# Graph layer with relation weights: three of every 66 gather tiles fetched row by row instead of two, with byte offsets and 32 registers per load

## The chip, the cores and the metric

The kernel runs on one core of a Trainium2 chip. Its time is the device time of one launch, in microseconds: the median of three runs of the kernel before is 10409.57 us (10406.67 to 10411.6). The profiled execution of the same kernel took 10414.85 us.

## The reference

A graph has 12,500 nodes of 64 features and 412,500 edges, sorted by destination; every edge has one of 65 types. A first layer sums normalised source rows per destination. Then the relational part runs twice:

```python
seg = dst * r + edge_type
msg = x[src]
agg = segment_sum(msg, seg).reshape(n, r, d)
mean = agg / maximum(cnt, 1.0)
out = einsum('nrd,rdk->nk', mean, W_r) + x @ W_root + b
h = relu(out) + relu(h @ res_W + res_b)
```

The kernel multiplies first and gathers afterwards: for every node it writes the rows of x W_r for all 65 types (and the root and residual products) into a table in HBM, `y_table`. An edge then needs one row of 64 floats (256 bytes) of this table, at row `src * 67 + type`. A one-hot matrix weighted by 1/count adds the rows of a tile of 128 edges into their destinations on TensorE.

## The kernel before, in words

There are three passes: `l = 0` is the first graph layer, `l = 1` and `l = 2` are the gather passes of the two relational layers. The change concerns `l = 2`, which here is called layer 2 (`ROW_LAYER = 2`). In it nothing is multiplied by relation weights any more; it only gathers and sums.

The edges are cut into 98 steps (`S = 98`) of 33 tiles (`T = 33`), a tile being 128 edges. A step has three groups (`J = 3`, index `j`) of 11 tiles (`K = 11`, index `k`). Two steps make a pair, `i` is the pair, `u = 0` or `1` the step within it, and all engines loop over pairs. The buffers of `u = 0` are called `rows` in the trace, those of `u = 1` lie in a weight buffer and are called `w_parts`. So there are six groups of buffers, and each group is refilled once in a pair.

- GpSimd (POOL) fetches tiles: one `indirect_dma_start` (line 878) takes 128 rows by the indices in `idx_st`. It may fill a group's buffers when TensorE is through with them (`agg_done`) and the indices lie ready (`idx_staged`).
- One tile in each step, the last one of the first group (`j = 0`, `k = ROW_K = 10`), is not fetched by GpSimd (`pool_tiles`). Its 128 indices are loaded into one partition (`load_row_idx`, line 299). Then SyncE (SP) or ScalarE (ACT) reads 16 of them into registers (line 305, a TENSOR_LOAD) and issues 16 transfers of one row each (line 309), and so on (`load_rows`). SP does this for the tile of `u = 0`, half of it in either step of the pair; ACT does it for the tile of `u = 1`, in the same way.
- ACT also copies the sums of the step before out of PSUM (line 987), and stages the indices for GpSimd two steps ahead (line 982, `stage_ahead`), each group when TensorE has used the group's buffers.
- TensorE (PE, line 1436) waits for a group's gathers and, at the row-by-row tile, for `rows_landed`; then it does 11 matmuls, which the trace counts as 22 since they are of f32. After a step's first group it turns the sums of the step before (line 1270), and VectorE (DVE) finishes that block (lines 1675 to 1684).
- SP also loads the root and residual product of each block (`load_rr`, line 563).

SP's queue for one pair (`sp_step`) is: load the row indices of the next pair; load `rr`; wait for the first group of this step and for the indices; 64 rows; `rr`; 64 rows. ACT's (`act_step`) is, in each step: copy the sums, then stage and issue rows in turn, 64 rows a step.

Of the kernel before, what the change touches and what calls it, by code (L numbers as in the profile page):

```python
# [5 lines left out]
P = 128  # L6
# [39 lines left out]
def gnn_kernel(nc, N, E, R, D, x, src, dst, etype, rel_W, root, bias, res_W, res_b,  # L46
# [4 lines left out]
    f32, bf16, i32 = mybir.dt.float32, mybir.dt.bfloat16, mybir.dt.int32  # L51
# [10 lines left out]
    J = 3  # L62
# [22 lines left out]
    ROW_BATCH = 16  # L85
    ROW_HALF = P // 2

# [31 lines left out]
    with ctx:  # L119
# [172 lines left out]
        row_idx = [extra[0:1, u * P:(u + 1) * P] for u in range(2)]  # L292

        def pool_tiles(l, j, tiles):
            return [k for k in range(tiles) if not (l == ROW_LAYER and j == 0 and k == ROW_K)]

        def load_row_idx(eng, pair, u):
            at = (pair * 2 + u) * T + ROW_K
            eng.dma_start(row_idx[u].rearrange("p (e a) -> p e a", a=1),
                          col_table[1:2, :, bass.ds(at, 1)], allow_slow_non_contiguous=True)\  # L300
               .then_inc(row_idx_loaded[u], 16)

        def load_rows(eng, which, l, u, r0, n):
            for c0 in range(r0, r0 + n, ROW_BATCH):
# [107 lines left out]
        rows_landed = [sem(f"rows_landed{u}") for u in range(2)]  # L412
        row_idx_loaded = [sem(f"row_idx_loaded{u}") for u in range(2)]
# [65 lines left out]
        def _(sp):  # L479
# [101 lines left out]
            with sp.If(in_windows == 1):  # L581
# [53 lines left out]
                for l in (1, 2):  # L635
# [11 lines left out]
                    if l == ROW_LAYER:  # L647
                        wait_alone(sp, agg_done[l], 1)
                        load_row_idx(sp, 0, 0)
                        wait_alone(sp, row_idx_loaded[0], 16)  # L650
                        load_rows(sp, mybir.EngineType.SP, l, 0, 0, P)

                    def sp_step(i, u, more):
# [6 lines left out]
                        def next_rows(n):  # L660
                            if more:
                                load_rows(sp, mybir.EngineType.SP, l, 0, u * ROW_HALF + n * ROW_BATCH, ROW_BATCH)

                        if more and u == 0:
                            load_row_idx(sp, i + 1, 0)
# [5 lines left out]
                        if more and u == 0:  # L671
                            wait_alone(sp, agg_done[l], s * J + 2 * J + 1)
# [1321 lines left out]
```

## Time and profile before

| | |
|---|---|
| median of three runs | 10409.57 us |
| the profiled execution | 10414.85 us, of which the span of the program is 10412.8 us |
| POOL busy | 7664.3 us, 74% |
| DVE, PE, ACT busy | 52%, 44%, 22% |
| DMA in layer 2 | 16% of the 16 engines' time, 30 GB/s |
| layer 2 | from 6497 us to the end |

A POOL row of the profile is 0.94 us long and another follows 0.30 us later, without pause; this gap is shown as "issue", time in which the engine waits for nothing that the trace records. Instructions that set registers, branch, wait on a semaphore or issue a transfer are not counted as busy, so an engine can have its queue full and look idle. They do have records, under SPq and ACTq (the queues of SyncE and ScalarE); FUSED_REGOPS is register arithmetic, MOVE sets one register, DMA_DIRECT2D issues one transfer and TENSOR_LOAD reads memory into registers.

### The profile page before, as it was taken

The numbers are of one execution on the slowest core, as the hardware profiler recorded it, in microseconds if no ns is written. First come the engines' busy times: TensorE is split into PE (matmuls) and PEld (weight loads), VectorE is DVE, ScalarE is ACT, GpSimd is POOL, SyncE is SP. The second block draws the span as 40 slices with busy tenths as digits, with TensorE's granted clock in tenths as the row PEclk, the third lists the DMA queues.
The fourth block names the chain that finished last, engine by engine and source line by source line (L and its number), as shares of the span: only waits on it lengthen the run. The fifth ranks groups of instructions, "written<-read, shape, count | busy, mean of one in ns | idle before, by whom it ended". The sixth has DMA issues, their size and how long they took to land.

```text
span 10412.8 us, 180513 instructions
## 1 busy us (share of the span) xinstructions
PE 4552.2 (44%) x39273; PEld 3351.5 (32%) x39273; DVE 5439.9 (52%) x20234; ACT 2260.0 (22%) x5671; POOL 7664.3 (74%) x8196
## 2 busy tenths in 40 slices
PE   4489898885444444444444444222222222222222
PEld 3366666663222222222222222122222222222222
DVE  9877676766766766766776776222222222222222
ACT  7756565652111111111111111000000000000000
POOL 6577777775777777777777776777777777777777
PEclk8889999996666666666666666555555555555555
DMA  3234444445444444444444444111111111111112
GB/s 88 60 129 147 139 147 140 146 138 166 147 146 138 146 142 142 146 141 144 142 143 145 140 144 146 30 30 30 30 30 30 30 30 30 30 30 30 30 30 41
DMA packets 517848, 1018.14 MB, mean 98 GB/s; under 512 B 224773, under 2 KB 270869, under 8 KB 516309
## 3 DMA queue, kind: packets, MB, share of 16 engines
q1 hardware_dynamic: 242628, 745.04, 19.6%
q0 software_dynamic: 254784, 263.18, 13.0%
q14 instruction: 662, 5.42, 0.2%
q10 hardware_dynamic: 19600, 1.66, 0.1%
q8 instruction: 174, 2.85, 0.1%
HBM read 559.40 MB, written 454.23 MB: 97 GB/s over the span
## 4 chain that ended last, share of the span: by engine, by line
POOL 60%; issue 23%; PE 8%; DVE 4%; SPq 2%; ACT 1%; DMA 1%; POOLq 0%; ACTq 0%; DVEq 0%
POOL rows L878 33%; POOL w_parts L878 27%; PE y_ps L1241 3%; PE block_ps L1328 2%; DVE ystage L1569 2%; SPq L309 1%; PE sums_ps L1293 1%; PE y_ps L1320 1%; ACT scr L1016 1%; SPq L305 0%; PE signs_ps L1320 0%; DMA y_table<-ystage 0%; ACTq L309 0%; DVE onehot L1604 0%; DMA rows<-h_table,idx_st 0%
## 5 line engine op out<-in xcount | busy, mean ns | idle before, releaser
L878 POOL DMA_INDIRECT rows<-y_table,idx_st x3185 | 3009.1, 945 | 1052.4 <-issue 1051.8
L878 POOL DMA_INDIRECT w_parts<-y_table,idx_st x3163 | 2986.9, 944 | 964.5 <-issue 964.5
L1675 DVE TENSOR_SCALAR rr<-rr 128x64 f32<-128x64 f32 x198 | 43.4, 219 | 4125.0 <-PE block_ps L1270 4125.0
L1436 PE MATMUL sums_ps<-onehot,rows 128*64 128x64 f32 x6468 | 762.2, 315 | 2669.9 <-DMA rows<-y_table,idx_st 2537.8
L1436 PE MATMUL sums_ps<-w_parts 128*64 128x64 f32 x6424 | 754.6, 315 | 2583.7 <-DMA w_parts<-y_table,idx_st 2505.4
L878 POOL DMA_INDIRECT rows<-h_table,idx_st x1452 | 1399.0, 964 | 552.6 <-issue 453.5
L1436 PEld LDWEIGHTS sums_ps<-onehot,rows 128*64 128x64 f32 x6468 | 710.7, 225 | 2748.8 <-issue 1320.4
L1436 PEld LDWEIGHTS sums_ps<-w_parts 128*64 128x64 f32 x6424 | 707.4, 225 | 2658.0 <-issue 2169.1
L982 ACT ACTIVATE idx_st<-edges 128x11 int32 (+1 forms) x720 | 141.3, 210 | 5850.9 <-PE sums_ps L1436 3218.2
L1006 ACT ACTIVATE ystage<-y_ps 128x512 f32<-128x512 f32 (+1 forms) x1782 | 1010.7, 568 | 977.5 <-PE y_ps L1241 819.6
L1614 DVE TENSOR_SCALAR_CACHE_REDUCE w_raw<-edges,step_key 128x384 bf16<-128x384 f32 x1568 | 850.8, 606 | 15.6 <-DVE step_key L1594 15.6
L1241 PE MATMUL y_ps<-scr,hT 128*128 128x512 bf16 (+1 forms) x2673 | 741.0, 421 | 64.8 <-ACT hT L992 54.4
L1606 DVE TENSOR_SCALAR onehot<-iota,step_rel,step_val 128x64 f32<-128x64 bf16 x3234 | 755.4, 335 | 21.9 <-PE sums_ps L1260 5.0
L1606 DVE TENSOR_SCALAR w_parts<-iota,step_rel,step_val 128x64 f32<-128x64 bf16 x3234 | 755.8, 339 | 12.3
L1241 PE MATMUL y_ps<-w_parts,hT 128*128 128x512 bf16 (+1 forms) x2673 | 705.8, 375 | 36.2 <-ACT ystage L1006 18.6
L1328 PE MATMUL block_ps<-edges,scr 128*128 128x192 bf16 x5346 | 602.2, 251 | 0.0
L1328 PEld LDWEIGHTS block_ps<-edges,scr 128*128 128x128 bf16 x5346 | 540.9, 139 | 174.9 <-issue 16.4
L1614 DVE TENSOR_SCALAR_CACHE_REDUCE w_raw<-w_raw,step_key 128x384 bf16<-128x384 f32 x784 | 425.2, 607 | 0.0
L1241 PEld LDWEIGHTS y_ps<-scr,hT 128*128 128x128 bf16 x2673 | 253.2, 111 | 528.0 <-issue 224.9
L1016 ACT ACTIVATE scr<-y_ps 128x396 bf16<-128x396 f32 x864 | 385.5, 498 | 129.2 <-PE y_ps L1320 115.4
L970 ACT ACTIVATE ystage<-iota,w_parts 128x128 bf16<-128x128 bf16 x1176 | 343.7, 385 | 3.0 <-PE signs_ps L1213 2.8
L1569 DVE TENSOR_TENSOR ystage<-t_ps,edges 128x896 bf16<-128x896 bf16 x588 | 343.9, 665 | 0.7 <-DVE win_cnt L1559 0.4
(230 smaller groups left out, 6414.8 us busy)
## 6 DMA issues: line engine op xcount, KB each, us to landing
y_table<-ystage SPq DMA_DIRECT2D x396, 768.0 KB, 3.7
edges<-key_row SPq DMA_DIRECT2D x198, 832.0 KB, 6.3
y_table<-ystage SPq DMA_DIRECT2D x198, 608.0 KB, 3.3
w_parts<-y_table ACTq DMA_DIRECT2D x6272, 0.2 KB
rows<-y_table SPq DMA_DIRECT2D x6272, 0.2 KB
w_raw<-key_row SPq DMA_DIRECT2D x99, 832.0 KB, 7.1
rows<-y_table,idx_st POOLq DMA_INDIRECT x3185
w_parts<-y_table,idx_st POOLq DMA_INDIRECT x3163, 2.5
```

The costliest lines, as they stand in the source:

```text
L309: eng.dma_start(rows_of(l, u)[r:r + 1, 0, ROW_K, 0:D], y_table[l - 1][bass.ds(value, 1), :])\
L878: pool.indirect_dma_start(out=rows_of(l, u)[:, j, k, 0:D], out_offset=None, in_=table, in_offset=bass.IndirectOffsetOnAxis(ap=idx_of(l, u, ...
L970: ins = nc.scalar.activation(hist_oh[:, v, K - SIGNS + a, 0:P], iota[:, 0:P], ACT.Sign, bias=lo_half[:, bass.ds(q * SIGNS + a, 1)], scale= ...
L982: nc.scalar.activation(idx_of(l, u, j), of, ACT.Copy).then_inc(idx_staged[l], 1)
L1006: nc.scalar.activation(ystage[:, n % 2, o:o + y_cols(c)], y_ps[c % 2][:, 0:y_cols(c)], ACT.Copy).then_inc(y_read[l], 1)
L1016: nc.scalar.activation(counts_at(half, f), hist_ps[f % 2][half][:, 0:FC * NBK], ACT.Copy)\
L1241: ins = nc.tensor.matmul(y_ps[c % 2][:, 0:n], hT[:, v, a // 2, :], parts_of[l][:, a, c * BANK:c * BANK + n], start=a == 0, stop=a == 2 and ...
L1328: ins = nc.tensor.matmul(block_ps[:, 0:3 * D], counts.rearrange("p (n h) -> p h n", h=NBK)[:, b, :], h_cols[:, b, :], start=b == 0, stop=b ...
L1436: ins = nc.tensor.matmul(sums_ps[u][0:width, c:c + W], rows_of(l, u)[:, j, k, 0:width], onehot_of(l, u)[:, j, k, :], start=False, stop=False)
L1569: ins = V.tensor_tensor(hist_oh[:, v, 0:k, c0:c1].rearrange("p k (n b) -> p k n b", b=2), iota_ps[:, 0:2 * n].rearrange("p (n b) -> p n b" ...
L1606: ins = V.tensor_scalar(to, iota[:, 0:W], step_rel[:, s_par[0], at], step_val[:, s_par[0], at], ALU.is_equal, ALU.mult)
L1614: ins = V.tensor_scalar(at, key_b[j][:, k * P:(k + 3) * P], step_key[:, s_par[0], j * K + k:j * K + k + 1], None, ALU.is_equal, ALU.add, a ...
```

## The change

Three tiles per pair come row by row in layer 2: one for `u = 0` as before and two for `u = 1`, the last and the last but one of the first group (`ROW_KS`). They are numbered `n`: 0 and 1 as before, 2 is the new one. In each step SP and ACT issue 96 rows each. SP has all of `n = 0` and the first half of `n = 2`, ACT all of `n = 1` and the second half of `n = 2`.

The indices are multiplied by 256 on ScalarE beforehand (`place_rows`), and the transfers are addressed in a view of bytes, so the register that was loaded is the offset. One load fills 32 registers. SP now waits for ACT's `row_placed` where it waited for the index load, and in the pair's second step it waits for `agg_done` too. GpSimd takes the last tile of each group first, and in the very last tile only the 89 rows that are needed; both of these hold in all layers.

```diff
     ROW_K = K - 1
-    ROW_BATCH = 16
+    ROW_BYTES = 4 * D
+    ROW_BATCH = 32
     ROW_HALF = P // 2
+    ROW_STEP = 3 * ROW_BATCH
+    ROW_KS = (K - 1, K - 2)
...
+        def pool_tiles(l, u, j, tiles):
+            by_rows = ROW_KS[:1 + u] if l == ROW_LAYER and j == 0 else ()
+            return [k for k in range(tiles) if k not in by_rows]
...
+        def place_rows(n, loaded):
+            wait_alone(nc.scalar, row_idx_loaded[n], loaded * 16)
+            nc.scalar.activation(row_at[n], row_idx[n], ACT.Copy, scale=float(ROW_BYTES))\
+              .then_inc(row_placed[n], 1)
+
+        def load_rows(eng, which, l, n, r0, rows, k=ROW_K):
+            u = min(n, 1)
+            for c0 in range(r0, r0 + rows, ROW_BATCH):
                 _, values = nc.values_load_multi_w_load_instructions(
-                    row_idx[u][:, c0:c0 + ROW_BATCH], engines=[which], min_val=0, max_val=NBK * P * RX - 1,
+                    row_at[n][:, c0:c0 + ROW_BATCH], engines=[which], min_val=0,
+                    max_val=(NBK * P * RX - 1) * ROW_BYTES,
                     skip_runtime_bounds_check_because="sources are clamped to the table, types lie below R")
                 for r, value in enumerate(values, c0):
-                    eng.dma_start(rows_of(l, u)[r:r + 1, 0, ROW_K, 0:D], y_table[l - 1][bass.ds(value, 1), :])\
-                       .then_inc(rows_landed[u], 16)
+                    eng.dma_start(rows_of(l, u)[r:r + 1, 0, k, 0:D].bitcast(u8),
+                                  y_bytes[l - 1][:, bass.ds(value, ROW_BYTES)]).then_inc(rows_landed[n], 16)
...
                     def sp_step(i, u, more):
...
                         if more and u == 0:
-                            load_row_idx(sp, i + 1, 0)
+                            for n in (0, 2):
+                                load_row_idx(sp, n, i + 1, min(n, 1), ROW_KS[n // 2])
...
                         load_rr(l, s + 1, 1 - u)
-                        if more and u == 0:
-                            wait_alone(sp, agg_done[l], s * J + 2 * J + 1)
-                            wait_alone(sp, row_idx_loaded[0], i * 16 + 32)
-                        next_rows(0)
...
+                        if more:
+                            wait_alone(sp, agg_done[l], s * J + 2 * J + 1)
+                            wait_alone(sp, row_placed[2 * u], i + 2)
+                            if u == 0:
+                                load_rows(sp, mybir.EngineType.SP, l, 0, 0, ROW_STEP)
+                            else:
+                                load_rows(sp, mybir.EngineType.SP, l, 0, ROW_STEP, P - ROW_STEP)
+                                load_rows(sp, mybir.EngineType.SP, l, 2, 0, ROW_HALF, ROW_KS[1])
...
                         read_sums(l, s, 1 - u)
+                        if l == ROW_LAYER and u == 0 and more:
+                            place_rows(0, i + 2)
+                            load_row_idx(act, 1, i + 1, 1)
                         stage_ahead(0)
                         next_rows(0)
...
                         if l == ROW_LAYER and u == 0 and more:
-                            load_row_idx(act, i + 1, 1)
+                            for n in (1, 2):
+                                place_rows(n, i + 2)
+                            for n in (1, 2):
+                                wait_alone(act, row_placed[n], i + 2)
```

The start of SP's loop over pairs in layer 2, before. `edges` holds the row indices in one partition; ISA is register arithmetic or a wait's set-up:

```order
L687 ISA
L299 DMA edges<-col_table 1x128x1
L669 ISA
L563 ISA
L563 DMA rr<-y_table 128x128
L475 ISA x2
L305 TENSOR_LOAD edges
L309 ISA
L309 DMA rows<-y_table 1x64
```

The last two rows come 16 times behind each TENSOR_LOAD, which comes 8 times in the loop. The same place now, down to the second load:

```order
L701 ISA
L306 DMA edges<-col_table 1x128x1
L306 ISA
L306 DMA edges<-col_table 1x128x1
L684 ISA
L578 ISA
L578 DMA rr<-y_table 128x128
L490 ISA
L490 REGISTER_ALU
L318 TENSOR_LOAD edges
L323 DMA rows<-y_table 1x256 x32
L318 TENSOR_LOAD edges
```

The register arithmetic ahead of each row's transfer is gone, there is a second load of indices, and 32 transfers stand behind each of now 6 TENSOR_LOADs in the loop. The start of ACT's loop over pairs, now (`agg_t` takes the sums, L312 is `place_rows`, L998 stages the indices for GpSimd):

```order
L1003 ACTIVATE agg_t<-sums_ps 65x256
L490 ISA
L312 ACTIVATE edges<-edges 1x128
L306 ISA
L306 DMA edges<-col_table 1x128x1
L1140 REGISTER_ALU
L998 ISA
L998 ACTIVATE idx_st<-edges 128x11
L318 TENSOR_LOAD edges
L323 DMA w_parts<-y_table 1x256 x32
```

Before, the L987 copy was followed at once by the staging; the wait for SP's indices (L490), the multiplication and ACT's own index load now stand between them. GpSimd's loop in layer 2, where the first groups of `u = 0` and `u = 1` are the rows with 10 and 9, before them 10 and 10:

```order
L894 DMA rows<-y_table,idx_st 128x64 x10
L490 REGISTER_ALU
L894 DMA rows<-y_table,idx_st 128x64 x11
L490 REGISTER_ALU
L894 DMA rows<-y_table,idx_st 128x64 x11
L490 ISA
L894 DMA w_parts<-y_table,idx_st 128x64 x9
```

One gather in 64 has left the loop.

## Rows read from the trace of the kernel before

**Rows 1.** The page's part 4: shares of the chain of waits, by engine.
```profile
POOL 60%; issue 23%; PE 8%; DVE 4%; SPq 2%; ACT 1%; DMA 1%; POOLq 0%; ACTq 0%; DVEq 0%
```

**Rows 2.** Line 878 in layer 2: duration ns min/median/max, first and last start us.
```profile
L878 POOL DMA_INDIRECT rows<-y_table,idx_st x1568: 940/944/1028, 6498.2 to 10375.8; - x196
L878 POOL DMA_INDIRECT w_parts<-y_table,idx_st x1557: 940/944/1015, 6538.2 to 10402.1; - x195
  issue: 979.6, 3123
```

**Rows 3.** Timeline of SP's queue over a pair: start us, us, what, count.
```profile
8035.71 30.83 SPq L309 DMA_DIRECT2D rows<-y_table  x64
8066.82 0.36 SPq L563 DMA_DIRECT2D rr<-y_table  x1
8068.64 30.92 SPq L309 DMA_DIRECT2D rows<-y_table  x64
8102.57 0.61 SPq L299 DMA_DIRECT2D edges<-col_table  x1
8103.49 0.37 SPq L563 DMA_DIRECT2D rr<-y_table  x1
8115.73 4.42 SPq L309 DMA_DIRECT2D rows<-y_table  x10
```

**Rows 4.** Timeline of ACT and its queue in the same stretch.
```profile
8034.15 0.38 ACT L987 ACTIVATE agg_t<-sums_ps 65x256 f32<-65x256 f32 x1 [10.56 <-PE sums_ps L1436]
...
8035.73 6.00 ACTq L309 DMA_DIRECT2D w_parts<-y_table  x16
8048.16 0.21 ACT L982 ACTIVATE idx_st<-edges 128x11 int32 x1 [13.53 <-PE sums_ps L1436]
```

**Rows 5.** Line 309 by operation; below, who waited for its rows.
```profile
L309 ACTq FUSED_REGOPS  x6272: 37/37/37, 6500.7 to 10388.6; - x196
L309 ACTq DMA_DIRECT2D w_parts<-y_table x6272: 213/213/929, 6500.8 to 10388.8; - x196
L309 SPq FUSED_REGOPS  x6272: 37/37/47, 6501.1 to 10338.4; - x196
L309 SPq MOVE rows<-y_table x6272: 29/29/38, 6501.2 to 10338.4; - x196
L309 SPq DMA_DIRECT2D rows<-y_table x6272: 224/225/374, 6501.2 to 10338.5; - x196
...
  PE sums_ps L1436: 203.1, 10
```

**Rows 6.** Line 299, the index load: issues and the MOVEs ahead of them.
```profile
L299 SPq DMA_DIRECT2D edges<-col_table x49: 572/599/628, 6497.6 to 10261.5; - x49
L299 SPq MOVE edges<-col_table x48: 29/29/30, 6564.0 to 10261.4; - x48
```

**Rows 7.** Line 305, loads of 16 registers.
```profile
L305 ACTq TENSOR_LOAD <-edges x392: 1047/1202/4130, 6499.6 to 10381.5; - x196
L305 SPq TENSOR_LOAD <-edges x392: 1139/1230/1388, 6499.9 to 10330.5; - x196
```

**Rows 8.** Line 580, SP's load of one register.
```profile
L580 SPq TENSOR_LOAD <-flag x1: 922/922/922, 451.2 to 451.2; - x1
```

**Rows 9.** Line 1010, ACT's load of one register.
```profile
L1010 ACTq TENSOR_LOAD <-flag x1: 1127/1127/1127, 445.6 to 445.6; - x1
```

**Rows 10.** Timeline of SP's queue at the start of layer 2.
```profile
6497.62 0.60 SPq L299 DMA_DIRECT2D edges<-col_table  x1
6501.21 62.61 SPq L309 DMA_DIRECT2D rows<-y_table  x128
6564.10 0.63 SPq L299 DMA_DIRECT2D edges<-col_table  x1
```

**Rows 11.** Timeline at the end: TensorE's last group, and the last store.
```profile
10404.79 2.58 PE L1436 MATMUL sums_ps<-w_parts 128*64 128x64 f32 x22 [10.32 <-DMA w_parts<-y_table,idx_st]
...
10410.31 0.48 SPq L766 DMA_DIRECT2D out<-x_sb  x1
```

More of the change, by code:

```diff
@@ L290, in idx_of @@
             return idx_st[:, u * J + j, :]
[L292 to L299, printed above, removed]
-                          col_table[1:2, :, bass.ds(at, 1)], allow_slow_non_contiguous=True)\
-               .then_inc(row_idx_loaded[u], 16)
@@ L303, in load_rows @@
-        def load_rows(eng, which, l, u, r0, n):
-            for c0 in range(r0, r0 + n, ROW_BATCH):
+        row_idx = [extra[0:1, n * P:(n + 1) * P] for n in range(3)]
+        row_at = [extra[0:1, (3 + n) * P:(4 + n) * P] for n in range(3)]
+        y_bytes = [t.rearrange("(o n) d -> o (n d)", o=1).bitcast(u8) for t in y_table]
+        def pool_tiles(l, u, j, tiles):
+            by_rows = ROW_KS[:1 + u] if l == ROW_LAYER and j == 0 else ()
+            return [k for k in range(tiles) if k not in by_rows]
@@ L411, in gnn_kernel @@
         gathered = [[[sem(f"gathered{l}{u}{j}") for j in range(J)] for u in range(2)] for l in range(3)]
-        rows_landed = [sem(f"rows_landed{u}") for u in range(2)]
-        row_idx_loaded = [sem(f"row_idx_loaded{u}") for u in range(2)]
+        rows_landed = [sem(f"rows_landed{n}") for n in range(3)]
+        row_idx_loaded = [sem(f"row_idx_loaded{n}") for n in range(3)]
+        row_placed = [sem(f"row_placed{n}") for n in range(3)]
         idx_staged = [sem(f"idx_staged{l}") for l in range(3)]
@@ L658, in next_keys @@
                             load_keys(s * J + J + j, j)
-                        def next_rows(n):
-                            if more:
-                                load_rows(sp, mybir.EngineType.SP, l, 0, u * ROW_HALF + n * ROW_BATCH, ROW_BATCH)
                         if more and u == 0:
-                            load_row_idx(sp, i + 1, 0)
+                            for n in (0, 2):
+                                load_row_idx(sp, n, i + 1, min(n, 1), ROW_KS[n // 2])
                         if l == 1:
@@ L670, in sp_step @@
                         load_rr(l, s + 1, 1 - u)
[L671 to L674 removed]
                         if l < 2:
[L676 to L680 removed]
+                            save_y(l, s, u, range(YG - 1))
                         if l == 1:
@@ L876, in gather_group @@
                         wait_alone(pool, agg_done[l], q + 1)
-                        for k in pool_tiles(l, j, tiles):
+                        ks = pool_tiles(l, u, j, tiles)
+                        for k in ks[-1:] + ks[:-1]:
+                            n = END_ROWS if isinstance(s, int) and (s * J + j) * K + k == (E - 1) // P else P
                             pool.indirect_dma_start(
-                                out=rows_of(l, u)[:, j, k, 0:D], out_offset=None, in_=table,
-                                in_offset=bass.IndirectOffsetOnAxis(ap=idx_of(l, u, j)[:, k:k + 1], axis=0))\
+                                out=rows_of(l, u)[0:n, j, k, 0:D], out_offset=None, in_=table,
+                                in_offset=bass.IndirectOffsetOnAxis(ap=idx_of(l, u, j)[0:n, k:k + 1], axis=0))\
                                 .then_inc(gathered[l][u][j], 16)
@@ L1098, in _ @@
                     if l == ROW_LAYER:
+                        for n in (0, 2):
+                            place_rows(n, 1)
                         for slot in range(2):
@@ L1108, in act_step, with next_rows @@
                         more = not isinstance(s, int) or s + ahead < S
-                        ready = [False]
-                        def next_rows(n):
+                        def next_rows(b):
                             if l == ROW_LAYER and (more or u == 0):
-                                if u and not ready[0]:
-                                    ready[0] = True
-                                    wait_alone(act, row_idx_loaded[1], i * 16 + 32)
-                                load_rows(act, mybir.EngineType.Activation, l, 1,
-                                          (1 - u) * ROW_HALF + n * ROW_BATCH, ROW_BATCH)
+                                if u:
+                                    n, r0 = 1, b * ROW_BATCH
+                                else:
+                                    n, r0 = ((1, ROW_STEP), (2, ROW_HALF), (2, ROW_HALF + ROW_BATCH))[b]
+                                load_rows(act, mybir.EngineType.Activation, l, n, r0, ROW_BATCH, ROW_KS[n // 2])
                         def stage_ahead(j):
```

41 lines of the change are left out of this document (22 added, 19 removed).

## The prediction

> **What bounds the kernel now.** I read the page first, its shares of the chain of waits. POOL carries 60% of the span, and the 23% of "issue" are its 0.30 us pauses: nothing else matters much over the whole kernel [rows 1]. Then the one line of POOL in layer 2: 1568 + 1557 = 3125 gathers, the first starting at 6498.2 and the last ending at 10402.1 + 0.94 = 10403.0. That is 1.2495 us per gather, 64 gathers and 80.0 us per pair of steps, and of all idle time ahead of them practically everything is "issue" [rows 2]. So layer 2 is GpSimd's gather rate from end to end. Every gather less in a pair is worth 1.25 us x 49 pairs = 61.2 us, if POOL stays what comes last.
>
> Whether it stays is told by the queue that will now do more. SP's queue in one pair: 64 rows in 30.83 us, `rr`, 64 rows in 30.92, 3.0 us for the loop's return (8099.56 to 8102.57), index load, `rr`, and then nothing from 8103.86 until shortly before 8115.73 [rows 3]. The last load of registers ahead of 8115.73 took 1.2 us, so SP waited about 10.6 of 80.0 us and worked 69.4. This is the figure that the change must fit under 78.7 us (63 gathers). ACT's queue is lighter: it does the same 128 rows at 0.37 to 0.39 us each and sits waiting for TensorE before it stages indices [rows 4]. TensorE waited for rows that came one by one only 10 times, 203 us, all at the start of the layer [rows 5].
>
> **The cost of one row on SP.** From the first row at 8035.71 to the `rr` behind it at 8066.82 there are 31.11 us, with 64 rows, 3 more register loads of 1.23 us [rows 7] with a gap of 0.035, and about 0.24 for `rr`'s own registers. That leaves 27.07 us, 0.423 per row. Its parts: FUSED_REGOPS 0.037, MOVE 0.029, DMA_DIRECT2D 0.225 [rows 5], and 0.132 in three gaps of 0.044. The byte offsets take away the FUSED_REGOPS and one gap: 0.423 - 0.081 = **0.342 us**. The MOVE stays. It isn't the arithmetic: index loads have it for 48 of 49 issues, all but the first, whose address is fixed [rows 6], so it belongs to a transfer with an offset in a register, and these still have one. Bounds of the row: 0.335 from the medians alone, 0.350 if the gap that goes is a short one.
>
> **The cost of one load of 32 registers.** No row shows it. 16 registers take 1.230 us on SP and 1.202 on ACT [rows 7], one takes 0.922 on SP [rows 8] and 1.127 on ACT [rows 9]. The steeper line, SP's, adds 16 x 0.0205 = 0.33 and gives 1.56; a flat cost gives 1.23, and less than that no row gives a reason for. I take the middle, **1.39**. From the other side, if all of it were per register, it would be 2 x 1.23 = 2.46.
>
> **SP's turn over one pair, after.** In each step 96 rows: 96 x 0.342 + 3 x (1.39 + 0.035) = 37.1 us. The turn is then
> - return of the loop 3.0;
> - from the issue of the index load to the first row load 2.8: 2.3 until the indices have landed (issue at 6497.62, first register load at 6499.9 [rows 10, 7]), then ACT's new multiplication, a small activation like the 0.21 of line 982 [rows 4], with some 0.25 for two hand-overs. The second index load (0.9) and `rr` (0.65) lie inside these 2.8. Before, the landing lay under the 10.6 us of waiting; that cover is gone now;
> - 37.1, `rr` 0.7, two waits 0.2, and 37.1 again.
>
> The sum is **80.9 us**. The same sum with the old figures (3.0 + 1.3 + 0.1 + 32.1 + 0.7 + 32.1 = 69.3) gives the 69.4 measured above. So SP needs 80.9 us for what POOL now does in 63 x 1.2495 = 78.7, and 80.0 before. The likeliest outcome is that the bound moves from POOL to SP's queue and the pair gets 0.9 us longer instead of 1.25 shorter.
>
> Does anything else hold it up? ACT issues rows at (6.00 - 0.213) / 15 = 0.386 [rows 4, 5], less 0.037 and a gap of 0.036 = 0.313; three times 32 rows and a load are 34.3 us a step. In the first step of a pair ACT starts 2.8 us behind SP's index load (it must multiply it first), so its last rows of the second tile of `u = 1` go out at about 39 and TensorE is through with that group at about 41, just when SP asks for it (2.8 + 37.1 + 0.7 = 40.6). This costs SP 0 to 0.5 us. Queued behind ACT's new wait is the staging of GpSimd's indices; POOL has six groups of room, 78.7 us, so it fills in behind. The reordering of tiles within a group costs nothing, since TensorE waits for the whole group's gathers before it begins; the smaller last tile saves at most part of two gathers, some 1 us.
>
> **The sum over the layer.** SP starts at 6497.6; 2.8 for indices; 128 rows and 4 loads 49.5; 64 rows and 2 loads 24.7; so its loop begins at 6574.9. 47 turns of 80.9 bring the last one to 10377.2. From there the end hangs on ACT: 41 until the second step's group, 35 for its next rows and 35 + 2 for the last ones with their landing, 113 in all. Then 1.2 to turn the block and what follows the start of TensorE's last group now, 10412.8 - 10404.8 = 8.0 [rows 11]. Together 10499.4, which is 86.6 over the span of 10412.8. The profiled execution takes 2.05 us more than its span and the median of the runs lies 5.3 below it: 10409.6 + 86.6 = **10496 us**. One us of the turn is 48 us of the kernel. The bounds of row and load (0.335 with 1.23, 0.350 with 1.56 and the 0.5 from ACT) give turns of 78.6 and 83.5, and times of 10385 and 10620: the forecast's own range.
>
> **Rivals.**
> 1. *POOL stays the bound.* The turn must be under 78.66 us, a row under 0.330. What could do it: the transfer itself gets cheaper without an address to scale (ACT has 0.213 where SP has 0.225, so the 0.225 isn't a floor), or the MOVE goes as well (0.342 - 0.073 = 0.269, turn 66.9). Against it: the 48 of 49 above. Then 61.2 us are saved, less 2.5 at the start: ACT can stage the seventh group only behind SP's first index load of the loop (6574.9 + 2.8 + 1.2 = 6578.9), and POOL is there at 6576.9. Time 10409.6 - 61.2 + 2.5 = **10351**.
> 2. *A tie.* Turns of 78.66 to 79.53 give a time within 0.2% (21 us, about what a measurement of this kernel can tell from no change).
> 3. *A load costs by the register:* 2.46 us, six of them per turn, 6 x 1.07 = 6.4 us more, 48 x 6.4 = 308: **10804**. Against it: one register took 75% to 94% of what 16 took.
> 4. *256 one-byte elements cost SP what a larger shape does:* the 128-row `rr` issue takes 0.37 [rows 3] where a row takes 0.225. 192 x 0.14 = 27 us a turn: about **11,790**.
>
> That the change doesn't do what it says I exclude: the built order shows no arithmetic between transfers and 6 loads where 8 were.
>
> The Trainium skill speaks on two of these, beside the sums above. Its page "Runtime: NRT & Kernel Launch", section "Instruction fetch mechanics", puts a TENSOR_LOAD at about 200 ns per register even in bulk. This case's trace disagrees: 16 registers would take 3.2 us and take 1.23. By the page 32 would take 6.4 us and the kernel some 11,900 us. The page "DMA: Bandwidth & Descriptors", section "Issuing engines are not separate DMA queues", says that issuing from several engines saves only the sequencers' issue time, usually small beside the DMA itself. By that the issue time would not matter and rival 1 would hold; the trace has SP at 69.4 of 80.0 us with almost nothing but issue.
>
> **How the numbers follow.** The forecast (SP comes last, slower by more than 0.2%) 0.55; rival 1 0.30; rival 2 0.08; rivals 3 and 4 together 0.07. The margin between SP and POOL, 2.2 us of 80.9, is 0.012 us a row, and I know the row no better than to 0.01, so the gain keeps a good part. Faster 0.30, same 0.08, slower 0.62. The range goes from rival 1 with a little below it, 10345, to 10600, within the forecast's own 10385 to 10620; it leaves out rivals 3 and 4 and the upper end, about 0.13.
>
> **What would show it.** Under the forecast: row periods on SPq of 0.34, no FUSED_REGOPS at the transfers but a MOVE; SP's turn 81 us with no wait over 1 us; loads of 1.3 to 1.5 us; TensorE waiting once a pair for rows rather than for gathers; POOL with a pause of some 2 us or more in each pair, waiting for `idx_st` or TensorE. A turn of 78.7 with SP waiting for TensorE says rival 1. The prediction is wrong in its core if POOL never pauses in layer 2.

## The result and the profile after

| | before | changed |
|---|---|---|
| median | 10409.5 us (4 runs, 10406.7 to 10411.6) | 10983.5 us (4 runs, 10981.4 to 10989.5) |
| ratio | | 1.0552, 95% interval 1.0536 to 1.0568 |
| profiled execution, span | 10412.8 us | 10981.6 us |
| one pair of steps in layer 2, median | 79.8 us | 90.6 us |

The prediction was 10496 us, with a range from 10345 to 10600. The sign and the place were right: SP's and ACT's queues take the bound from GpSimd. The size was not: +574 us where +87 were forecast.

A pair's time is read here, and in every kernel below, as the median distance between SP's index loads of one pair and the next. There are 47 such distances in SP's loop, so 1 us of it is 47 us of the kernel.

The page's shares of the chain of waits, after:

```profile
POOL 32%; issue 20%; ACTq 18%; SPq 12%; PE 8%; DVE 4%; DMA 4%; ACT 1%; DVEq 0%; POOLq 0%
```

It answers to [rows 1]: POOL fell from 60% to 32%, and the two queues together went from 2% to 30%. The 4% of DMA are transfers that something waits for; before it was 1%.

Line 894, GpSimd's gathers in layer 2, after:

```profile
L894 POOL DMA_INDIRECT rows<-y_table,idx_st x1568: 938/944/1013, 6495.4 to 10879.8; - x196
L894 POOL DMA_INDIRECT w_parts<-y_table,idx_st x1508: 938/944/2039, 6535.3 to 10912.8; - x189
  issue: 915.1, 2863
  ACT idx_st L998: 608.9, 210
```

A gather costs what it did [rows 2]; new is 609 us of waiting for `idx_st`, the indices that ACT stages between its rows. GpSimd is now the one that waits.

Line 323 by operation, and who waited for it:

```profile
L323 ACTq DMA_DIRECT2D w_parts<-y_table x9408: 213/222/952, 6502.7 to 10968.9; - x196
L323 SPq MOVE rows<-y_table x6272: 29/29/38, 6499.6 to 10896.1; - x196
L323 SPq DMA_DIRECT2D rows<-y_table x6272: 224/228/654, 6499.7 to 10896.2; - x196
  PE sums_ps L1461: 2244.6, 98
```

Against [rows 5] the FUSED_REGOPS are gone and the MOVE stayed, as predicted. An issue takes ACT 222 ns where it took 213. TensorE waited 98 times for rows, twice in each of 49 pairs, and not 10 times.

Line 318, the loads of 32 registers:

```profile
L318 SPq TENSOR_LOAD <-edges x294: 2025/2123/2308, 6497.5 to 10909.4; - x147
L318 ACTq TENSOR_LOAD <-edges x294: 1990/2141/2314, 6500.6 to 10956.9; - x147
```

Here the forecast had 1.39 us, from 1.23 for 16 and 0.92 for one [rows 7, 8]. SP's queue over one pair:

```profile
8023.69 1.34 SPq L306 DMA_DIRECT2D edges<-col_table  x2
8025.33 0.38 SPq L578 DMA_DIRECT2D rr<-y_table  x1
8030.39 37.36 SPq L323 DMA_DIRECT2D rows<-y_table  x96
8068.02 0.37 SPq L578 DMA_DIRECT2D rr<-y_table  x1
8075.47 10.71 SPq L323 DMA_DIRECT2D rows<-y_table  x32
8088.59 23.86 SPq L323 DMA_DIRECT2D w_parts<-y_table  x64
8115.22 1.32 SPq L306 DMA_DIRECT2D edges<-col_table  x2
```

It answers to [rows 3]. This pair takes 8115.22 - 8023.69 = 91.5 us, 0.9 more than the median. A row's period in its block of 32 is (10.71 - 0.228) / 31 = 0.338 us. Between the second `rr` and the next 32 rows SP stands from 8068.4 to 8075.5; a load of registers takes 2.1 of that, some 4.7 are a wait for TensorE. ACT in the same stretch, where the number in brackets is the idle time ahead and what ended it:

```profile
8027.80 0.31 ACT L312 ACTIVATE edges<-edges 1x128 int32<-1x128 int32 x1 [2.93 <-DMA edges<-col_table]
...
8031.10 10.53 ACTq L323 DMA_DIRECT2D w_parts<-y_table  x32
...
8057.32 10.50 ACTq L323 DMA_DIRECT2D w_parts<-y_table  x32
8067.96 0.51 ACT L312 ACTIVATE edges<-edges 1x128 int32<-1x128 int32 x2 [12.66 <-issue]
8068.72 0.38 ACT L1003 ACTIVATE agg_t<-sums_ps 65x256 f32<-65x256 f32 x1 [0.25 <-ACT edges L312]
8073.32 0.21 ACT L998 ACTIVATE idx_st<-edges 128x11 int32 x1 [4.22 <-PE sums_ps L1461]
```

And TensorE, which waits for both queues' rows:

```profile
8072.48 0.69 PE L1461 MATMUL sums_ps<-w_parts 128*64 128x64 f32 x4 [37.31 <-DMA w_parts<-y_table]
...
8089.90 0.48 PE L1461 MATMUL sums_ps<-onehot,rows 128*64 128x64 f32 x2 [6.63 <-DMA rows<-y_table]
```

Read the three together. ACT's last row goes out at 8057.32 + 10.50 = 8067.82, and TensorE gets to work with it at 8072.48, **4.66 us later**. SP's last row of `u = 0` is out at 8086.18 and used at 8089.90, 3.7 us later. The forecast had ACT's last rows out at 39 and TensorE through with the group at 41, 2 us with the matmuls in them. The index load issued at 8023.69 is used at 8027.80, 4.1 us later, where it had 2.3. Each is on a ring, a chain of waits that comes back to its start once a pair: index load, ACT's 96 rows, landing, TensorE, then SP's and ACT's next rows.

### The profile page after: what moved, and what is told of

Read it like the earlier page. It is cut to its first block, busy times and chain, and to the rows that moved or that the text cites. A ratio compares the mean times of both kernels' runs of the same rounds, so it can differ in the third digit from the quotient of the medians.

```text
span 10981.6 us, 180901 instructions
## 1 busy us (share of the span) xinstructions
PE 4526.2 (41%) x39273; PEld 3311.9 (30%) x39273; DVE 5429.7 (49%) x20234; ACT 2301.4 (21%) x5818; POOL 7617.7 (69%) x8147
## 3 DMA queue, kind: packets, MB, share of 16 engines
q8 instruction: 174, 2.85, 0.1%
## 4 chain that ended last, share of the span: by engine, by line
POOL 32%; issue 20%; ACTq 18%; SPq 12%; PE 8%; DVE 4%; DMA 4%; ACT 1%; DVEq 0%; POOLq 0%
POOL rows L894 18%; ACTq L323 14%; POOL w_parts L894 13%; SPq L323 9%; ACTq L318 3%; PE y_ps L1266 3%; PE block_ps L1353 2%; SPq L318 2%; DMA w_parts<-y_table 2%; DVE ystage L1594 2%; DMA edges<-col_table 1%; PE sums_ps L1318 1%; ACT scr L1032 1%; PE y_ps L1345 1%; PE sums_ps L1461 1%
## 5 line engine op out<-in xcount | busy, mean ns | idle before, releaser
L894 POOL DMA_INDIRECT w_parts<-y_table,idx_st x3114 | 2942.3, 945 | 1227.8 <-issue 920.1
L998 ACT ACTIVATE idx_st<-edges 128x11 int32 (+1 forms) x720 | 141.5, 210 | 5719.0 <-issue 2505.0
L1295 PE MATMUL block_ps<-ident,agg_t 64*128 64x64 f32 (+1 forms) x972 | 250.4, 406 | 1213.8 <-ACT agg_t L1003 1204.7
L1295 PEld LDWEIGHTS block_ps<-ident,agg_t 64*128 64x128 f32 (+1 forms) x972 | 208.0, 298 | 1246.5 <-ACT agg_t L1003 1214.4
```

What stands on the lines that cost most here:

```text
L894: pool.indirect_dma_start(out=rows_of(l, u)[0:n, j, k, 0:D], out_offset=None, in_=table, in_offset=bass.IndirectOffsetOnAxis(ap=idx_of(l, ...
L1295: ins = nc.tensor.matmul(block_ps[:, 0:width], agg_t[0:width, b, o:o + P], ident[0:width, 0:width], start=n == 0, stop=n == len(halves) - 1)
```

## The experiments

**Theory A**, formed on this trace: GpSimd's 78.6 us are no longer what comes last. A ring is, through the index load, both queues and two landings, and the landings are late because two queues' rows arrive faster (one each 0.17 us) than they land. **Rivals**: byte transfers are slow in themselves (B, E); 32 registers at a time is the mistake (C, D); SP's queue alone is the bound; one of the two queues alone is.

The ratios are to the kernel before, measured again beside each group of runs (10409 to 10415 us). Of each edit below only the core is shown.

| kernel | time, us | ratio, 95% interval | one pair, us |
|---|---|---|---|
| before | 10412 | 1 | 79.8 |
| changed | 10983 | 1.0552 (1.0536 to 1.0568) | 90.6 |
| two_bytes | 10414.7 | 1.0003 (0.9993 to 1.0012) | 79.9 |
| batch16 | 10939.6 | 1.0508 (1.0486 to 1.0529) | 89.5 |
| late_wait | 10840.3 | 1.0412 (1.0391 to 1.0433) | 87.5 |
| early_idx | 10813.9 | 1.0387 (1.0366 to 1.0408) | 87.3 |
| both_mends | 10821.4 | 1.0393 (1.0362 to 1.0423) | 87.4 |
| both_16 | 10876.1 | 1.0445 (1.0415 to 1.0475) | 88.5 |
| sp_only | 10593.8 | 1.0174 (1.0144 to 1.0203) | 83.2 |
| sp_only_16 | 10684.9 | 1.0262 (1.0243 to 1.0280) | 85.1 |
| act_only | 10468.8 | 1.0050 (1.0032 to 1.0069) | 80.6 |
| old_address | 11456.2 | 1.1002 (1.0970 to 1.1034) | 99.9 |
| no_third | 10356.2 | 0.9942 (0.9927 to 0.9957) | 78.6 |
| five_of_four | 10644.7 | 1.0218 (1.0204 to 1.0232) | 83.6 (two take 167.2) |
| five_early | 10393.2 | 0.9981 (0.9972 to 0.9990) | 79.3 (two take 158.7) |

### two_bytes: the third tile taken back, bytes and loads of 32 kept

```diff
-    ROW_STEP = 3 * ROW_BATCH
-    ROW_KS = (K - 1, K - 2)
+    ROW_STEP = 2 * ROW_BATCH
+    ROW_KS = (K - 1,)
```

> The changed kernel without its third tile: byte offsets, ACT's multiplication and 32 registers per load stay, 64 rows a step on SP and ACT each as before. Theory A (the loss comes from the amount of work on two queues that wait for each other): SP's turn is 128 x 0.341 + 4 x 2.12 + some 8 = 60 us, ACT's is alike, both well under GpSimd's 64 gathers = 80.0 us, so 10410 us, within 15. Rival B (transfers by bytes, or the 32-register loads, slow down the gathers themselves): over 10430 us, with a gather period above 1.25 us.

Measured 10414.7: the new form of transfer costs nothing while GpSimd has the longer turn. All of the 574 us hang on the third tile. Its rows land late already: from the last issue of a block to the last landing there are 3.6 us on SP and 3.1 on ACT (medians; before has 1.7 and 1.5). Here the slack of both queues covers it.

### batch16: the changed kernel with 16 registers at a time

```diff
-    ROW_BATCH = 32
+    ROW_BATCH = 16
```

The shares of the work stay: 96 rows a step and queue, which ACT still issues 32 at a time between its stagings.

> The changed kernel with 16 registers per load, so 12 loads of 1.23 us instead of 6 of 2.12 us on each queue in a pair. Theory A (three loads on ACT and three on SP lie one behind the other on the path of a pair): 6 x (2 x 1.23 - 2.12) = 2.0 us more per pair, 48 x 2.0 = +98, so about 11080 us. Rival C (the one DMA engine that takes all single rows sets the pace, the loads lie beside it): 10983 within 20. Rival D (a load costs by the register and only the batch as a whole counts, 16 registers near 1.06 here): same as C, but with loads of 1.06 in the trace.

Measured 10939.6, 44 us faster than the changed kernel, which none of the theories had. Its loads were as before the change:

```profile
L318 SPq TENSOR_LOAD <-edges x588: 1140/1229/1486, 6498.9 to 10866.4; - x196
```

So 12 loads a pair cost more than 6 did, and rival D's 1.06 is out. TensorE and the two queues tell where it came back:

```profile
8014.55 38.00 SPq L323 DMA_DIRECT2D rows<-y_table  x96
8042.19 11.67 ACTq L323 DMA_DIRECT2D w_parts<-y_table  x32
8056.71 0.69 PE L1461 MATMUL sums_ps<-w_parts 128*64 128x64 f32 x4 [36.03 <-DMA w_parts<-y_table]
```

ACT's last row is out at 8053.86 and used at 8056.71, 2.85 us later and not 4.66. The index load issued at 8010.43 is used at 8012.87, 2.4 us later and not 4.1. The rows are spread out more by the loads between them (96 in 38.0 us instead of 37.4), so less piles up. The DMA queues show it too. These are q10, which carries ACT's transfers, in the stretch 7000 to 10000 us (packets, MB, share of 16 engines' time) of before, of the changed kernel and of batch16:

```profile
q10 hardware_dynamic: 15078, 1.27, 0.3%
```

```profile
q10 hardware_dynamic: 17462, 1.67, 1.1%
```

```profile
q10 hardware_dynamic: 17752, 1.69, 0.4%
```

As many packets as in batch16 took almost three times as long: 1.1% of 16 x 3000 us are 528 us, 30 ns a packet, where before's take 10. So there are not more packets but slower ones; where they wait is told at the end of the account of the prediction.

### late_wait, early_idx, both_mends: are the waits the cost?

late_wait puts SP's two waits of the odd step behind the 32 rows that don't need them; they stood ahead of these rows:

```diff
                             else:
                                 load_rows(sp, mybir.EngineType.SP, l, 0, ROW_STEP, P - ROW_STEP)
+                                wait_alone(sp, agg_done[l], s * J + 2 * J + 1)
+                                wait_alone(sp, row_placed[2], i + 2)
```

early_idx issues the index loads of the pair after next behind SP's last register load:

```diff
+                if ahead and c0 + ROW_BATCH >= r0 + rows:
+                    ahead()
...
-                        if more and u == 0:
-                            for n in (0, 2):
-                                load_row_idx(sp, n, i + 1, min(n, 1), ROW_KS[n // 2])
```

> The changed kernel, but SP waits for the second step's group (agg_done) and for the third tile's offsets behind the 32 rows of its own tile, which don't need them, and not ahead. Theory A (each pair is a ring ACT rows, landing, TensorE, SP rows, index load): SP's 4.7 us of waiting go, and what is left is ACT's own turn, 91.5 - 2.9 of idling for indices = 88.6 in the stretch read, 2.9 less: 48 x 2.5 to 2.9, so 10845 to 10865 us. Rival C (the pace is set by the DMA engine that takes single rows) or SP's queue being the bound by itself: 10983 within 20, the wait turning up at another place.

> The changed kernel, but SP issues the two index loads of the pair after next behind its last register load of a pair, some 11 us earlier, not at the head of the next. Theory A: ACT no longer idles 2.9 us for indices, SP not 2.2; ACT's own turn of 88.6 us is left, as in the kernel with the late wait: 10845 to 10865 us. Rival (SP's queue alone is the bound): SP wins 2.2 us per pair, 48 x 2.2 = 106, so 10877, with ACT idling at another wait. Rival C: 10983 within 20.

> Both small repairs together: SP's two waits in the odd step stand behind the 32 rows that don't need them, and the index loads of the pair after next are issued behind the last register load of SP's turn. Theory A (two engines hand rows to one place that lands them; a ring through the landing, TensorE and ACT's own queue sets the turn): SP is no longer late, but ACT's queue is full by itself: 192 rows at 0.33 us and 6 loads of 2.12 us are 76 us, with its own work (copies of sums, staged indices) and the 4.4 us in which it waits for TensorE about 87 us a pair, as early_idx alone has it. Expected 10800 (10775 to 10830). If SP's queue by itself were the bound, the two repairs would add up: 10983 - 143 - 170 = 10670 (10640 to 10700).

Measured 10840.3, 10813.9 and 10821.4. Each takes over 3 us out of a pair, and together they take no more than one: 87.5, 87.3, 87.4. A ring explains that; SP's queue alone would have given 10670 for both, and rival C 10983. early_idx lies 31 us under the 10845 expected: its first pairs are shorter (69, 81 and 84 us between loads, where late_wait has 80, 84 and 88). What then is left is ACT's own queue. ACT in both_mends, one pair, and TensorE:

```profile
8006.66 0.38 ACT L1007 ACTIVATE agg_t<-sums_ps 65x256 f32<-65x256 f32 x1 [0.25 <-ACT edges L312]
8011.43 0.21 ACT L1002 ACTIVATE idx_st<-edges 128x11 int32 x1 [4.38 <-PE sums_ps L1465]
8013.68 10.52 ACTq L325 DMA_DIRECT2D w_parts<-y_table  x32
...
8094.09 0.38 ACT L1007 ACTIVATE agg_t<-sums_ps 65x256 f32<-65x256 f32 x1 [0.25 <-ACT edges L312]
```

```profile
8010.59 0.69 PE L1465 MATMUL sums_ps<-w_parts 128*64 128x64 f32 x4 [34.69 <-DMA w_parts<-y_table]
```

It takes 7.0 us from the copy of the sums to its next row, 4.4 of it waiting for TensorE, which waits for the landing of ACT's own rows: the last is out at 8005.77 and used at 8010.59.

### sp_only, act_only, sp_only_16: one queue by itself

Half of the rows of the row-by-row tiles are left out of the computation in each. Core of sp_only (act_only has SP in the place of ACT):

```diff
             u = min(n, 1)
+            if which == mybir.EngineType.Activation:
+                return
             for c0 in range(r0, r0 + rows, ROW_BATCH):
```

> ACT issues none of its rows and fills none of their registers, and TensorE waits for SP's rows alone, so half of the rows of the three tiles are left out of the computation; SP issues all that it issues in the changed kernel. Theory A (the landing is late because SP's and ACT's rows together arrive faster, one per about 0.17 us, than they land): with one queue alone they land as they are issued, SP's last row lands 1.6 to 2.2 us behind its issue, not 3.7; the index loads land in 2.3 us, not 4.1; the turn is SP's own queue, 91.5 - 2.2 - 4.7 = 84.6 us with hardly a wait, so 10983 - 47 x 6 to 7 = 10655 to 10715. Rival E (a transfer addressed in bytes lands late by itself): the landing stays at 3.7 us and more, and SP's turn near 88 us, 10840 to 10870. Rival F (ACT alone is the bound, SP's queue would fit under GpSimd's turn): GpSimd's 78.7 us of the pair show, 10400 to 10440.

> The counterpart of sp_only: SP issues none of its rows and TensorE waits for ACT's alone (half of the three tiles' rows are left out of the computation). Theory A: ACT's queue by itself is longer than GpSimd's turn too: 91.5 us less the 2.9 and 4.2 that it waited, less about 2 for rows that issue faster alone, plus some 2 to 3 for the landing of its own rows that it still waits out: 84.5 to 85.5 a pair, 10690 to 10740. Rival H (only SP's queue is too long, ACT just follows it): GpSimd's turn shows, 10400 to 10440.

> sp_only with 16 registers at a time: with one queue alone nothing piles up at the landing, so the load's own price shows. SP fills 192 registers a pair, by 6 loads of 2.02 to 2.31 us or by 12 of 1.23 to 1.29: 12.75 or 15.1 us. Theory A: the turn goes from 83.2 to 85.6 us, 10594 + 47 x 2.4 = 10705 (10690 to 10720), so the 44 us by which batch16 beat the changed kernel came from the landing alone. Rival (16 at a time is cheaper by itself, in what stands around a load): 10594 or below.

SP in sp_only, and then ACT (it only multiplies the indices) and TensorE:

```profile
8075.79 1.34 SPq L306 DMA_DIRECT2D edges<-col_table  x2
...
8080.62 36.17 SPq L325 DMA_DIRECT2D rows<-y_table  x96
8117.07 0.37 SPq L580 DMA_DIRECT2D rr<-y_table  x1
8119.85 10.68 SPq L325 DMA_DIRECT2D rows<-y_table  x32
8132.94 23.17 SPq L325 DMA_DIRECT2D w_parts<-y_table  x64
8159.14 1.31 SPq L306 DMA_DIRECT2D edges<-col_table  x2
```

```profile
8078.02 0.31 ACT L312 ACTIVATE edges<-edges 1x128 int32<-1x128 int32 x1 [70.88 <-DMA edges<-col_table]
...
8131.77 0.48 PE L1466 MATMUL sums_ps<-onehot,rows 128*64 128x64 f32 x2 [35.64 <-DMA rows<-y_table]
```

The last row of `rows` is out at 8130.53 and used at 8131.77: **1.24 us** where with both queues it was 3.7. The form of transfer is the same, so rival E is out: what makes the landing late is the second queue. The index load was used 2.2 us after its issue, at 8078.02, not 4.1. In act_only the same holds for ACT:

```profile
8019.69 9.88 ACTq L325 DMA_DIRECT2D w_parts<-y_table  x32
8030.56 0.69 PE L1466 MATMUL sums_ps<-w_parts 128*64 128x64 f32 x4 [28.71 <-DMA w_parts<-y_table]
```

It is 1.0 us from 8029.57 to 8030.56, and ACT's rows go out in 9.9 to 10.3 us per 32 instead of 10.4 to 10.9. Both queues by themselves are longer than GpSimd's 78.6 us: SP's 83.2, ACT's 80.6. So rivals F and H are out. In SP's 83.2 less than 1 us is left between its index issues, its `rr` and its register loads, and the kernel before takes 79.8: no repair of waits or landing could have made the three-tile form win. I had put ACT's queue at 84.5 to 85.5 (10690 to 10740 us), and 80.6 (10468.8 us) lies far under that: its rows became 3.4 us a pair faster (60.4 us for the six blocks of 32, 63.8 in the changed kernel) where I had allowed 2, and the landing of its own rows, for which I had added 2 to 3, held it up 0.6 us.

sp_only_16 takes 1.8 us a pair more than sp_only, somewhat less than the 2.4 expected (10684.9 us, 5 under the range): 16 at a time does cost more queue time. In batch16 the landing gave it back and more. With both_mends the balance tips again:

> both_mends with 16 registers at a time instead of 32: a load of 16 takes 1.23 to 1.29 us where one of 32 takes 2.12, so 6 loads more but 12.75 become 12 x 1.26 = 15.1 us, 2.4 us more a pair on each queue. Theory A with the late landing (rows spread out by the loads pile up less, as in batch16, where it was worth 3.3 us on the ring): 10983 - 170 to 180 - 44, so about 10765 (10740 to 10800). Without such a term: 10800 + 47 x 2.4 = 10913.

Measured 10876.1, 55 us slower than both_mends, between the two expectations and outside the range of 10740 to 10800. ACT's row after the copy of the sums says how much came back:

```profile
8033.65 0.21 ACT L1002 ACTIVATE idx_st<-edges 128x11 int32 x1 [2.61 <-PE sums_ps L1465]
```

It waited 2.6 us for TensorE where it waits 4.4 in both_mends. So the landing gave back 1.8 us a pair where I had put 3.3: in batch16 the ring went through the index load's landing too, and here it doesn't.

### old_address: three tiles with row numbers and the multiplication on the way

```diff
-                    eng.dma_start(rows_of(l, u)[r:r + 1, 0, k, 0:D].bitcast(u8),
-                                  y_bytes[l - 1][:, bass.ds(value, ROW_BYTES)]).then_inc(rows_landed[n], 16)
+                    eng.dma_start(rows_of(l, u)[r:r + 1, 0, k, 0:D],
+                                  y_table[l - 1][bass.ds(value, 1), :]).then_inc(rows_landed[n], 16)
```

`place_rows` then copies the indices without the factor 256.

> The changed kernel with the rows addressed as before (a row number in the register, multiplied on the way: one register operation more for each row), all else kept: three tiles, 32 registers at a time, the same waits. A row takes SP 0.42 us and ACT 0.39 instead of 0.34 and 0.33. Theory A: issue costs 96 x 0.08 + 96 x 0.06 = 13.4 us more on the ring of a turn, and the slower arrival takes the late landing away, 2 to 3 us for the rows and 1.5 to 1.8 for the indices: 8.6 to 9.9 us more a turn, 11390 to 11450. Rival E (the byte form itself lands late): nearly the same time, so this run tells by the landing alone; there both say 1.6 to 2 us. A rival without any landing term: 10983 + 47 x 13.4 = 11613.

Measured 11456.2, 6 us above theory A's 11390 to 11450 and far from the 11613 without a landing term. A pair is 9.3 us longer, though 192 rows cost SP 16 us more of queue (32 rows in 13.34 us instead of 10.7). SP, ACT and TensorE around the end of a step:

```profile
8035.77 12.18 ACTq L323 DMA_DIRECT2D w_parts<-y_table  x32
8050.16 0.69 PE L1461 MATMUL sums_ps<-w_parts 128*64 128x64 f32 x4 [42.70 <-DMA w_parts<-y_table]
8053.22 13.34 SPq L323 DMA_DIRECT2D rows<-y_table  x32
8068.10 0.48 PE L1461 MATMUL sums_ps<-onehot,rows 128*64 128x64 f32 x2 [6.97 <-DMA rows<-y_table]
```

The landings are 2.2 us (from 8047.95) and 1.5 us (from 8066.56): rows that are issued slower, one each 0.2 us from both queues together, pile up little. Byte offsets save more than they cost, and part of what they save is lost at the landing.

### no_third, five_of_four, five_early: what could be won

In no_third GpSimd leaves the third tile out and nobody fetches it; that part of layer 2's sums is left out of the computation.

```diff
-            by_rows = ROW_KS[:1 + u] if l == ROW_LAYER and j == 0 else ()
+            by_rows = (K - 1, K - 2)[:1 + u] if l == ROW_LAYER and j == 0 else ()
```

> GpSimd leaves the third tile out and nobody fetches it (that part of layer 2's sums is left out of the computation); two tiles a pair come by one-row transfers as in two_bytes. It is what the change could bring at best: theory A, 48 gathers of 1.25 us less: 10415 - 60 = 10355 (10345 to 10365). If another engine stood close behind GpSimd (TensorE or ACT), 10375 to 10410.

Measured 10356.2, as expected. The whole gain on offer was 0.58%, 1.2 us a pair, and the ring gave up 12.

five_of_four takes the third tile in every second pair only (`v = 1`); the loops run over two pairs.

```diff
-            by_rows = ROW_KS[:1 + u] if l == ROW_LAYER and j == 0 else ()
+            by_rows = ROW_KS[:1 + (u and not v)] if l == ROW_LAYER and j == 0 else ()
```

> A smaller dose: the third tile goes by one-row transfers in every second pair alone, so five tiles of each four steps, in bytes and by 32 registers; GpSimd issues 127 gathers per two pairs instead of 128. Theory A (a row's queue time on SP and ACT must fit under GpSimd's turn): SP needs 83 us in a pair with the third tile and about 61 in the next, 144 of GpSimd's 2 x 78, so GpSimd stays the bound and each gather left out gives 1.25 us: 24 x 1.25 = 30, so 10382 (10372 to 10400), faster than before by 0.2 to 0.4%. Rival G (each pair must fit by itself, since the rows of a step come only one turn ahead): the pair with three tiles takes 87 to 90 us and the other 78: 24 x 9 to 12 = 216 to 290 more, 10630 to 10700.

Measured 10644.7: my theory A missed and rival G had the number. But ACT's rows name a wait, and it is none of rival G's:

```profile
8064.23 0.38 ACT L1020 ACTIVATE agg_t<-sums_ps 65x256 f32<-65x256 f32 x1 [2.73 <-issue]
8087.27 0.31 ACT L313 ACTIVATE edges<-edges 1x128 int32<-1x128 int32 x1 [22.66 <-DMA edges<-col_table]
```

ACT stood 22.66 us with nothing to do, for an index load that stood in SP's queue behind 64 rows. So one line was moved:

```diff
                                 if v:
+                                    load_row_idx(sp, 0, i + 2, 0, ROW_KS[0])
                                     wait_alone(sp, agg_done[l], s * J + 2 * J + 1)
```

> five_of_four with one index load moved: that of the next pair (the two-tile one) stands before SP's 64 rows of the third tile and not behind them, since in five_of_four ACT waited 22.7 us for it in each second pair and SP's and ACT's next rows came late behind. Theory A' (a queue's rows must fit under GpSimd's two pairs together, as long as no index load stands behind rows that another queue waits for): SP 144 us of 157, ACT 127, GpSimd the bound again with 127 gathers: 10415 - 24 x 1.25 = 10385 (10372 to 10400). Rival G (each pair must fit by itself): still 87 to 90 us for the pair with three tiles, 10630 to 10650. In between (10450 to 10600): another wait of the same kind is left.

Measured 10393.2, ratio 0.9981 (0.9972 to 0.9990): rival G is out, and this version beats both kernels, if by 20 us; 10385 was expected, and its range of 10372 to 10400 holds. Two waits of GpSimd at the layer's start, 5.8 and 0.9 us, are part of the 8 us that are missing. GpSimd's waits in the stretch 7000 to 10000 us:

```profile
POOL rows L906 <- issue: 366.8, 1202, 0.3
POOL w_parts L906 <- issue: 365.0, 1196, 0.3
...
POOL rows L906 <- ACT idx_st L1017: 1.2, 4, 0.3
```

It waits for nothing but its own rate again. five_16, five_of_four with 16 registers at a time, has no time: there ACT issues only 64 of the 128 rows of its tile a pair, and TensorE would wait for the others for ever. It tells nothing of the theories.

## Why the prediction missed

Its steps for SP's turn, set against one pair of sp_only (SP's queue by itself) and of the changed kernel, all in us:

| step | predicted | sp_only | changed |
|---|---|---|---|
| loop's return | 3.0 | 3.0 | 2.8 |
| index load to the first register load | 2.8 | 2.7 | 4.5 |
| first 96 rows with 3 loads | 37.1 | 38.3 | 39.5 |
| `rr` and waits | 0.9 | 0.9 | 5.6 |
| second 96 rows with 3 loads | 37.1 | 38.4 | 39.1 |
| sum | 80.9 | 83.3 | 91.5 |

(The 2.16 us of a load stand between the rows that the timeline shows, and are counted with the 96 rows.)

- *That the bound moves from POOL to the queues, and TensorE then waits for rows*: right, shown by POOL's 609 us of waiting, by no_third and by the one-queue kernels. Rival 1, at 0.30, was far from it: even without any collision SP needs 83.2 us.
- *A row at 0.342*: right. The mean distance of two rows on SP over the layer is 0.333 alone (sp_only) and 0.340 with both queues. The MOVE stayed, for the reason given. Rival 4 is out.
- *A load of 32 registers at 1.39, bounds 1.23 to 1.56*: wrong. It is 2.12. In sp_only a load takes 2.15 us out of the rows' stream where the forecast had 1.43 with its gap, 4.3 us more a pair; with the rows' 1.8 and the index load's 0.1 less, that gives the 2.4 us by which 83.3 stands above 80.9. Two points, 1 and 16 registers, do not bound the third when the cost does not grow along a line. Rival 3's 2.46 was nearer than the forecast's bounds.
- *ACT costs SP 0 to 0.5 us; an index load lands in 2.3; ACT's last rows are out at 39 and TensorE is through with them at 41*: this is the step that failed, with 8.2 of the 10.6 us between 80.9 and the pair shown. I took the landings from a kernel in which they lay under slack and the queues issued slower, and held them fixed. From sp_only to the changed kernel the wait for ACT's rows and their landing adds 4.7 us (5.6 against 0.9), the landing of the indices 1.8 (4.5 against 2.7), slower rows and loads on SP 1.9, and the loop's return gives 0.2 back. The landing went from 1.2 us (one queue) to 3.7 and 4.7 (two), the index load's from 2.2 to 4.1. It isn't the landing alone: counted from SP's index load, ACT's last row is out at 44.1 and not at 39, and TensorE starts with it at 48.8.
- *ACT at 0.313 a row, 34.3 us a step*: right alone, too low beside SP. The mean distance over the layer is 0.316 in act_only and 0.334 in the changed kernel: 9.9 to 10.3 us per 32 rows against 10.4 to 10.9. With loads of 2.14 this makes ACT a bound of its own. both_mends and act_only differ by 6.8 us a pair: 63.5 us of rows against 60.4, and 7.0 us from the copy of the sums to the next row against 3.2.
- *One us of the turn is 48 us*: right. 9.7 x 48 = 466 of the 487 us missed.
- *Slips in the sums*: the upper bound of the turn comes to 83.5 without the 0.5 us from ACT that it names, so 84.0 and some 10644 us were meant; the loop begins at 6574.6 by the terms given, not 6574.9; and GpSimd's wait in rival 1, from 6576.9 to 6578.9, is 2.0 us and not 2.5. None changes the outcome: 90.6 lies above all of them.

Where do the rows pile up? The Trainium skill, "DMA: Bandwidth & Descriptors", section "Why a DMA increments its semaphore by 16 and not by 1", says that the slowest dimension longer than one decides over how many of the 16 engines a transfer is spread, that software may split a contiguous row so that it is spread too, that the hardware queues use the lowest-numbered engines, and that each engine that takes part reports its own landing. A row that isn't split would then always go to the same engine, whoever issues it. The trace agrees: ACT's 9408 rows are 9408 packets of 256 bytes, so none was split.

The trace's records of landings and packets place the backlog. An `rr` load reports 16 landings. Of the one issued 0.3 us behind the first 96 rows of a pair the fifteenth comes 1.5 us after the issue, and in the changed kernel the sixteenth comes 3.1 us after that (median of 40 loads); of the other `rr`, issued 4.5 us after the last row, it comes 0.07 us after. In before, sp_only and act_only the median is 0.05 us at most. So one engine of the sixteen is behind, and the other fifteen are not; all 16 together are busy 15% of the stretch from 7000 to 10000 us. While the backlog drains, the rows of the two queues land in turn, each queue's 0.36 us apart: one row each 0.18 us, where the two queues issue one each 0.17. From the last issue of a block to its last landing there are 5.0 us (median), in batch16 3.0, in act_only 1.2 and in sp_only 1.4. Of ACT's row packets between 6600 and 10300 us 1126 of 7827 took over 100 ns, with a median of 185 where 15 is usual; in act_only none did. The engine does not set the pace by itself, since 384 rows of 0.18 us are 69 us of a pair's 90.6; its delay counts because it stands on the ring.

What stays open is why a row's packet takes 185 ns there, and which engine it is: no run sent rows to another one.

## What to carry to other kernels

When work is moved from a full engine to a half-empty queue, add up that queue's whole turn against the full engine's new turn, and then ask of each latency in the sum whether it was measured under the load that the change brings: here the landing of a row went from 1.2 us to 3.7 and 4.7, and what the second queue brought cost 8.2 us a pair where the mis-sized load cost 4.3. Try a smaller share first. And look for the small load that another engine waits for behind a long block in the same queue: moving one such load was worth 252 us here (five_of_four against five_early).

## What was not expected of the hardware

- A TENSOR_LOAD into one register takes 0.92 us on SP (one load, from another tile), into 16 it takes 1.23, into 32 it takes 2.12 (294 loads, 2.03 to 2.31). The first 15 more registers cost 0.3 us, the next 16 cost 0.9.
- One-row transfers from two queues, one each 0.17 us together, are used 3.7 to 4.7 us after their issue; from one queue, one each 0.32 to 0.33 us, 1.0 to 1.2 us after it. Their issue slows as well, from 0.316 to 0.334 us on ACT.
- The backlog is on one DMA engine of 16: the sixteenth landing of an `rr` load behind such rows comes 3.1 us after the fifteenth, with one queue 0.02 to 0.05 us after it.
- Filling the registers in smaller lots, 1.8 us a pair dearer on an unshared queue, made the crowded kernel 44 us faster.
